# TensorE's loop rotated, with the pooled output products interleaved with the next window-strip's kv products, and the masked copies of v made on GpSimd

## The reference

```
qkv    = einsum(xw, qkv_w)                     # per 4x4 window, 384 channels
pooled = avg_pool5(qkv)                        # within the window
q, k   = relu(q), relu(k);  v = [v, 1]         # 32 heads of 8 channels: 16 full, 16 pooled
kv     = einsum('ngld,nglm->ngdm', k, v)       # per window and head, 8 x 9
out    = einsum('ngld,ngdm->nglm', q, kv)
out    = out[..., :-1] / (out[..., -1:] + 1e-15)
y      = bn(einsum(out, proj_w));  return x + y
```

## Time and profile before

| | us |
|---|---|
| median of three runs | 928.52 (928.47 to 930.1) |
| the profiled execution: its time | 930.24 |
| the profiled execution: its span, first to last instruction | 928.3 |
| mean granted TensorE clock, share of full speed | 0.993 |

### The profile page before, as it was taken

One profiled execution on the slowest core, in us unless ns is written; L12 is line 12 of the kernel. 1 busy time (PEld: TensorE's weight loads), 2 busy tenths in 40 slices (PEclk: granted clock), 3 DMA queues, 4 the chain that ended last, 5 costly groups with the idle time before them and its releaser, 6 DMA issues.

```text
span 928.3 us, 65376 instructions
## 1 busy us (share of the span) xinstructions
PE 873.8 (94%) x29282; PEld 733.4 (79%) x29282; DVE 772.3 (83%) x1625; ACT 609.5 (66%) x1542; POOL 456.0 (49%) x967
## 2 busy tenths in 40 slices
PE   0689999999999999999999999999999999999997
PEld 0578888888888888888888888888888888888885
DVE  7369989998878898998878998999887878787886
ACT  0457676767676767676766667676767676767673
POOL 1545454545454545555554545454545454545550
PEclk9999999999999999999999999999999999999998
DMA  9910000000000000000000000000000000000000
GB/s 378 431 50 17 26 17 26 17 26 17 25 19 25 26 17 26 17 26 17 26 17 26 18 26 17 26 17 27 17 26 17 25 25 18 26 17 26 18 26 27
DMA packets 15893, 38.77 MB, mean 42 GB/s; under 512 B 1888, under 2 KB 14688, under 8 KB 15456
## 3 DMA queue, kind: packets, MB, share of 16 engines
q1 hardware_dynamic: 15840, 38.26, 10.6%
HBM read 19.38 MB, written 18.87 MB: 41 GB/s over the span
## 4 chain that ended last, share of the span: by engine, by line
PE 93%; issue 3%; DVE 2%; POOL 1%; DMA 0%; ACT 0%; DVEq 0%; POOLq 0%
PE ps L611 23%; PE ps L582 19%; PE ps L538 14%; PE ps L549 9%; PE ps L556 9%; PE ps L633 7%; PE ps L627 6%; PE ps L635 4%; PE ps L558 4%; DVE stats L377 1%; DMA x_all<-x 0%; POOL hs L234 0%; DVE kvc_full L446 0%; POOL xp L234 0%; ACT o_sb L325 0%
## 5 line engine op out<-in xcount | busy, mean ns | idle before, releaser
L255 POOL TENSOR_TENSOR xn<-x_all,mean_t 128x384 f32<-128x384 f32 x96 | 79.4, 827 | 393.6 <-PE ps L558 375.1
L305 ACT ACTIVATE vm_pool<-ps,cst 128x256 f32<-128x256 f32 x576 | 225.5, 543 | 0.4 <-PE ps L549 0.4
L446 DVE TENSOR_TENSOR kvc_full<-ps,cst 128x864 f32<-128x864 f32 x192 | 193.7, 1050 | 17.8 <-PE ps L582 17.6
L446 DVE TENSOR_TENSOR kvc_pool<-ps,cst 128x864 f32<-128x864 f32 x192 | 193.2, 1048 | 0.0
L305 ACT ACTIVATE vm_full<-ps,cst 128x384 f32<-128x384 f32 x384 | 192.2, 598 | 0.9 <-PE ps L538 0.9
L312 ACT ACTIVATE q_full<-ps 128x384 f32<-128x384 f32 x96 | 47.2, 491 | 208.5 <-PE ps L556 208.5
L538 PE MATMUL ps<-wkv_sb,xn 128*128 128x128 f32 x1152 | 145.5, 276 | 23.5 <-POOL xn L256 23.5
L538 PEld LDWEIGHTS ps<-wkv_sb,xn 128*128 128x128 f32 x1152 | 144.1, 193 | 23.5 <-issue 23.5
L452 DVE SCALAR_TENSOR_TENSOR x_all<-ps,shift,x_all 128x384 f32<-128x384 f32 x96 | 59.3, 618 | 93.4 <-PE ps L633 93.2
L611 PEld LDWEIGHTS ps<-kvc_full,q_full 64*32 64x32 f32 x9216 | 99.5, 105 | 26.4 <-issue 26.3
L611 PE MATMUL ps<-kvc_pool,q_pool 64*32 64x72 f32 x9216 | 115.8, 230 | 2.1 <-issue 2.1
(11 more groups left out here) (66 smaller groups left out, 1242.2 us busy)
## 6 DMA issues: line engine op xcount, KB each, us to landing
out<-x_all SPq DMA_DIRECT2D x96, 192.0 KB, 1.9
x_all<-x SPq DMA_DIRECT2D x3, 4608.0 KB, 32.1
x_all<-x SPq DMA_DIRECT2D x6, 768.0 KB, 8.1
cst<-consts SPq DMA_DIRECT2D x1, 172.0 KB, 11.0
wkv_sb<-wkv SPq DMA_DIRECT2D x1, 128.0 KB, 10.8
o_sb<-proj SPq DMA_DIRECT2D x1, 128.0 KB, 10.4
wq_sb<-wq SPq DMA_DIRECT2D x1, 64.0 KB, 10.5
bn_sb<-bn SPq DMA_DIRECT2D x1, 2.0 KB, 10.3
```

What stands on the lines that cost most here:

```text
L255: link(pool.tensor_tensor(xr, src, mean, ALU.subtract), 1)
L305: last = act.activation(heads[:, :, e, :, 0:D], src, ACT.Copy, scale=col(mask + e))
L446: last = dve.tensor_tensor(kvc[:, g], src.to_broadcast(shape), own, ALU.mult)
```

## The change

1. TensorE's step is rotated. Before: kv(s), kv pooled(s), conv q(s), conv kv(s+1), transposes(s-1), conv kv pooled(s+1), project(s-1), out(s), out pooled(s). After: transposes(s-1), conv kv pooled(s+1), project(s-1), out(s), then out pooled(s) interleaved with kv(s+1), kv pooled(s+1), conv q(s+1), conv kv(s+2). The cyclic order is the same except for the interleaving. In it two of the six (tile, window) groups of the pooled output products (32 instructions) alternate with one tile of the full kv products (16 instructions), three times; the counts of `out_p` and `kv_f` come after the last of each.
2. The waits of that interleaved group are for `vm_f` of strip s+1 and for `y_done` of strip s-1. `y_done` no longer has its extra first count, so the strips that are waited for are the ones of before: kv(s+1) after the residual of s-1.
3. The loop of two steps is entered after steps 0 and 1 and left before steps 94 and 95, so that six step bodies stand in TensorE's program where there were four.
4. ScalarE copies full v once, to `v_full`; GpSimd makes the four masked copies from it (`masked_v`, 432 elements a partition each, the ones included), at the start of its step, ahead of `normalise_and_pool`. The pooled branch stays on ScalarE.
5. GpSimd normalises in one `tensor_scalar` instead of two `tensor_tensor`.
6. Two waits of TensorE for `km_p` and `vm_p` in `conv_q`, and a few others that later waits cover, are left out.

```diff
-                link(pool.tensor_tensor(xr, src, mean, ALU.subtract), 1)
-                pool.tensor_tensor(xn[:, p], xn[:, p], rstd, ALU.mult).then_inc(xn_ready, 1)
+                pool.tensor_scalar(xr, src, mean_t[:, s:s + 1], rstd_t[:, s:s + 1], ALU.subtract,
+                                   ALU.mult).then_inc(xn_ready, 1)
...
+            def masked_v(s):
+                pool.wait_ge(v_copied, s + 1)
+                wait(pool, kv_f, s)
+                for e in range(EF):
+                    last = pool.tensor_scalar(vm_full[:, :, e].rearrange("p t i c -> p t (i c)"),
+                                              v_full[:].rearrange("p t i c -> p t (i c)"), col(C_VF + e), None,
+                                              ALU.mult)
+                last.then_inc(vm_f, 1)
             def step(s, b, at, phase):
+                if not is_last(s):
+                    masked_v(s + 1)
...
+            def copy_v(s):
+                act.wait_ge(v_f, s + 1)
+                wait(act, vm_f, s)
+                act.activation(v_full[:].rearrange("p t i (h c) -> p t (i h) c", c=HC)[:, :, :, 0:D],
+                               ps[:, V_F, 0:TF * P].rearrange("p (t h m) -> p t h m", t=TF, m=D),
+                               ACT.Copy).then_inc(v_copied, 1)
...
+            def out_pooled_and_kv(s):
+                pe.wait_ge(vm_f, s + 2)
+                wait(pe, y_done, s)
+                pe.nop(nofuse=True)
+                groups = [(t, e) for t in range(TP) for e in range(WP)]
+                for i in range(TF):
+                    for t, e in groups[QG * i:QG * (i + 1)]:
+                        last = out_tile(True, t, e)
+                    if i == TF - 1:
+                        last.then_inc(out_p, 1)
+                    last = kv_tile(False, i)
+                last.then_inc(kv_f, 1)
...
             def step(s, p):
-                kv_products(s, False)
-                kv_products(s, True)
-                conv_q(s, p)
-                if not is_last(s):
-                    conv_kv(s + 1, 1 - p)
                 if not is_first(s):
                     transposes(s - 1)
                 if not is_last(s):
                     conv_kv_pooled(s + 1, 1 - p)
                 if not is_first(s):
                     project(s - 1)
-                out_products(s, False)
-                out_products(s, True)
+                out_products(s)
+                if is_last(s):
+                    out_products_pooled(s)
+                else:
+                    out_pooled_and_kv(s)
+                    kv_products_pooled(s + 1)
+                    conv_q(s + 1, 1 - p)
+                if not is_last(s) and not is_last(s + 1):
+                    conv_kv(s + 2, p)
```

More of the change, by code:

```diff
@@ L278, in _ @@
             normalise_and_pool(1, 1)
+            masked_v(0)
             over_strips(step)
@@ L293, in relu_k_pooled, with masked_v_pooled @@
                                ACT.Relu, scale=1 / 25.0).then_inc(km_p, 1)
[L295 to L301, removed]
-                heads = vm[:].rearrange("p t e i (h c) -> p t e (i h) c", c=HC)
-                src = ps[:, bank, 0:tiles * P].rearrange("p (t h m) -> p t h m", t=tiles, m=D)
-                for e in range(wins):
-                    last = act.activation(heads[:, :, e, :, 0:D], src, ACT.Copy, scale=col(mask + e))
-                last.then_inc(done, 1)
+            def copy_v(s):
[4 more added lines that the diff above has]
+                               ACT.Copy).then_inc(v_copied, 1)
+            def masked_v_pooled(s):
+                act.wait_ge(v_p, s + 1)
+                wait(act, kv_p, s)
+                heads = vm_pool[:].rearrange("p t e i (h c) -> p t e (i h) c", c=HC)
+                src = ps[:, V_P, 0:TP * P].rearrange("p (t h m) -> p t h m", t=TP, m=D)
+                for e in range(EP):
+                    last = act.activation(heads[:, :, e, :, 0:D], src, ACT.Copy, scale=col(C_VP + e))
+                last.then_inc(vm_p, 1)
             def relu_q(s):
@@ L587, in out_products, with kv_tile @@
-            def out_products(s, pooled):
-                q, kvc, done, bank, tiles, wins = (
-                    (q_pool, kvc_pool, out_p, OUTP, TP, WP) if pooled else
-                    (q_full, kvc_full, out_f, OUTF, TF, WF))
-                pe.wait_ge(qm_p if pooled else qm_f, s + 1)
-                pe.wait_ge(kvc_p if pooled else kvc_f, s + 1)
-                if not pooled:
-                    pe.wait_ge(kvc_p, s + 1)
-                elif not is_last(s):
-                    pe.wait_ge(km_f, s + 2)
-                    pe.wait_ge(vm_f, s + 2)
-                pe.nop(nofuse=True)
+            def kv_tile(pooled, t):
+                k, vm, bank, n = (k_pool, vm_pool, KVP, EP * KC) if pooled else (k_full, vm_full, KVF, EF * KC)
+                for r in range(G):
+                    rows = slice(H64 * r, H64 * (r + 1))
+                    for i in range(4):
+                        last = pe.matmul(ps[Q4 * i:Q4 * (i + 1), bank + r, t * n:(t + 1) * n],
+                                         k[rows, t, Q4 * i:Q4 * (i + 1)], vm[rows, t, :, i, :],
+                                         start=True, stop=True)
+                return last
@@ L614, in out_products @@
-                last.then_inc(done, 1)
+                for g in range(G):
+                    rows = slice(H64 * g, H64 * (g + 1))
+                    for c in range(4):
+                        r, w = c // QG, t * QG * wins + c % QG * wins + e
+                        last = pe.matmul(ps[Q4 * c:Q4 * (c + 1), bank + g, t * n:(t + 1) * n],
+                                         blocks[rows, 4 * t + c, Q4 * e:Q4 * (e + 1)], kvc[rows, r, w],
+                                         start=e == 0, stop=e == wins - 1)
@@ new lines, in out_tile, with kv_products, kv_products_pooled @@
+                return last
+            def kv_products(s):
+                wait(pe, y_done, s - 1)
+                pe.wait_ge(km_f, s + 1)
+                pe.wait_ge(vm_f, s + 1)
+                pe.nop(nofuse=True)
+                for t in range(TF):
+                    last = kv_tile(False, t)
+                last.then_inc(kv_f, 1)
+            def kv_products_pooled(s):
+                pe.wait_ge(vm_p, s + 1)
+                wait(pe, num_f, s)
+                pe.nop(nofuse=True)
+                for t in range(TP):
+                    last = kv_tile(True, t)
+                last.then_inc(kv_p, 1)
```

109 lines of the change are left out of this document (50 added, 59 removed).

## The result

| | before | after |
|---|---|---|
| median | 929.31 (928.47 to 931.02, 4 runs) | 1357.92 (1356.69 to 1360.28, 4 runs) |
| profiled span | 928.3 | 1356.0 |
| mean granted clock | 0.993 | 0.875 |

The ratio is 1.4606, 95% interval 1.458 to 1.4631: 46% slower, against a forecast of 919 us and a range that ended at 968. From here on a step is the distance between the starts of the q products of two strips in TensorE's timeline. From the fifth q products to the last there are 91 steps: (1342.13 - 99.85) / 91 = 13.65 us after, (914.32 - 78.12) / 91 = 9.19 before. They make 91 x 4.46 = 406 of the 427.7 us between the two spans; the fifth q products start 21.7 later (the first ones 7.9 later, and the four steps from there to the fifth 13.8 longer), and what follows the last is as long as before, 13.8 us against 13.9.

What follows compares the result with a forecast made beforehand. TensorE, busy 94% of the span, was taken as the bound. 36 steps at 9.05, 6 at 9.56 and 50 at 8.98 make 832.2 against 844.6; with 3 us for the start, 9.4 less: 919 us, range 905 to 968.

Steps and rivals of the forecast that it cites:

- M: Time of GpSimd's four masked copies of 432 elements: taken as 0.55 us each, 2.2 in all, bounds 1.60 to 3.72.
- third chain: Transposes, `to_image`, ScalarE's copy of v, GpSimd's masks, next interleaved group: 6.78 + M, 8.98 us a step.
- the forecast's own case of fast masks: Rival: with M up to 2.0 the residual binds, plain steps 8.81, those with statistics 9.05, time 911; chance 0.20.
- GpSimd becomes the bound: Rival: interleaved group waits for `vm_f` every step; 950 us at 0.65 an operation, 1053 at 0.93; chance 0.33.
- It now waits for two things that had a stage of 1.1 us more to spare before: Start of TensorE's interleaved group: its waits for the residual and the masks lose 1.1 us of slack.
- the 0.20 that ScalarE's pooled copies cost before: TensorE's wait for `vm_pool` ahead of kv pooled, 0.20 us every second step, expected to go as ScalarE loses 1.5.
- the hidden jump: TensorE's loop jump, behind 12 long conv kv instructions: priced 0 instead of 0.22 us a step.
- The normalise: GpSimd's two operations made one: loses 0.83 us, a handover and perhaps 0.5; strips 0 and 1 ready 2.2 earlier.
- The six bodies: Six cold step bodies in TensorE's program instead of four: about 1 us near the start, bounds 0 and 4.5.
- Steps with statistics: VectorE's loop through the residual, `out_p` and `own_heads`: 9.05 us in 36 steps, 9.56 in six with reductions.
- The interleaving: TensorE's pooled output and full kv products fill each other's gaps: 1.60 us for the group instead of 1.86.
- one of the rivals: Interleaving gains nothing, group 1.86 us: near 945 alone, near 928 with masks of 0.45; chance 0.08.

Runs made afterwards that it cites:

- e9_probe: The kernel before plus single GpSimd operations of 72, 432 and 864 elements behind its last strip, each waited for; 1020.38 us, one run.
- e2_tt_masks: The kernel after, with GpSimd's four masks made by `tensor_tensor` with the mask column broadcast instead of `tensor_scalar`; 1061.88 us, ratio 1.1415.
- e11_copies: The kernel after, with plain GpSimd copies in place of the masked ones, so window masking is left out; 935.66 us, ratio 1.0058.
- e4_masks_alone: The kernel before, with only the four full masked copies on GpSimd and one copy of v on ScalarE; 1405.81 us, ratio 1.5107.
- e1: The kernel after, with the four full masked copies made by ScalarE again, straight from PSUM; 937.27 us, ratio 1.0059.
- e5: e1 without interleaving: the pooled output products, then the full kv products; 931.83 us, ratio 1.0019.
- e6: e5 with the wait for the residual (`y_done`) moved behind the pooled output products; 929.76 us, ratio 0.9995.
- e10: e6 with `conv_kv` at the head of the step, so four step bodies stand in TensorE's program instead of six; 923.88 us, ratio 0.9936.
- e12_shared_masks: e10 with two of the four full masks on ScalarE and two on GpSimd by `tensor_tensor` with broadcast column; 893.67 us, ratio 0.9609.
- e13: e12_shared_masks with the interleaving put back and the wait for the residual behind the first third of the pooled output products; 904.36 us, ratio 0.9734.
- e8_late_mask_wait: The kernel after, with pooled output products in series waiting only for `v_copied`, and `vm_f` waited for ahead of the kv products; 1234.6 us, ratio 1.3274.

## Why the prediction was wrong

**The step that failed** is the price of M: "One input should need about the memset's time an element, and some of those 0.22 ... I take 0.55". It measured 1.367, outside its own bounds (0.40 to 0.93), so that M is 5.40 instead of 2.2. Both bounds came from other kinds of operation. The upper one took for granted that fewer inputs can't cost more than two, and e9_probe shows that they can: 1.37 against 1.09 at 432 elements. The Trainium skill's page "GPSIMD Engine Reference" has this order too (§ 4.1, as told in the prediction). The probe agrees for a copy (0.8 ns an element) and disagrees for `tensor_scalar` (2.5, more than `tensor_tensor`'s (2.00 - 1.09) / 432 = 2.1); by its § 3.1 I had estimated 0.65 for this operation, half of the measured.

**The form of the chain held,** with 0.2 too little in it. The forecast's third chain was 6.78 + M. Where the masks bind, e2_tt_masks gives 10.50 - 3.50 = 7.00, and after, less the 1.24 for the clock, 13.65 - 1.24 - 5.40 = 7.01. Most of the difference of 0.2 is the way from the interleaved group to q: 2.68 in e11_copies, where I had 1.60 + 0.90 = 2.50. At 7.00 + M the step is back at before's 9.19 with M = 2.19. So my own M of 2.2 would have given no gain: the steps of e11_copies that are shorter than 9.20 would have grown to it, 12.3 us together, which makes about 948 (an estimate from its 935.66 and its 91 steps).

**The price of M was not the only error.** With M = 2.02 the forecast's own case of fast masks has 911, and e11_copies took 935.66. Of these 25 us, the 45 plain steps at 9.00 instead of 8.81 make 9 and those with statistics 2; the fifth q products come 9.3 later than in before, where 3 was allowed; the last step of 11.87 makes 3, and the reduction steps about 5. Right masks alone would have left the change a little slower than before.

**The clock was in no case.** The 4.67 us between 13.65 and the forecast's 8.98 are 3.20 of M, 1.24 of the clock and 0.18 of the group; 0.05 is left over. The rival "GpSimd becomes the bound" named the mechanism, with 0.33, but its dearest figure was 1053 us at M = 3.72, and it held no loss of clock. Short of that loss it was near: for M = 3.50 its sum gives 1033, and e2_tt_masks, with that M and the clock at 1.00, came out at 1061.88.

**Slack that wasn't there, and a loop not seen.** "It now waits for two things that had a stage of 1.1 us more to spare before": true of the residual alone. `out_products` of before waits for `vm_f` of the next strip ahead of its pooled part (L601), and e4_masks_alone shows the stall there. And I counted the 0.20 that ScalarE's pooled copies cost before as a wait that the freed ScalarE would take away; with the masks on ScalarE it is a loop of 9.1 that holds every step of e1, e5, e6 and e10. That is why the rotation and the hidden jump bring so little by themselves: the mean step falls from 9.19 to ScalarE's 9.10, and the start, the end and the reductions take it back (e6_late_y_wait: same as before; e10_four_bodies: 0.6% faster). e12_shared_masks confirms the loop: with ScalarE's busy time 54 us lower over the run than in e10_four_bodies (555.9 against 609.7) the step is 8.75.

**The normalise** was taken as cheaper by more than half, with no effect other than at the start. Its 1654 ns equal the two old ones. The first kv products start at 37.52 instead of 30.09, 7.4 later where I had 2.0: 3.2 more of M, and 2.2 that I had credited to this operation.

**The six bodies** were priced at 1 us within bounds of 0 and 4.5. e10_four_bodies says 6, 2.2 of it in the last step, which I had called unchanged.

**What held:** the jump is hidden behind long matmuls (e1_act_masks has no alternation, where before had 9.06 and 9.31). The residual holds the plain steps once the masks are fast, 0.2 later than summed (9.00 in e11_copies against 8.81). Steps with statistics 9.05 forecast, 9.10 measured; with reductions 9.56 forecast, three steps of each image at 9.51 to 10.26 in e11_copies, so undersized. The forecast put the 0.80 of the earlier trace rows into six steps, but those rows count 4 such operations in the run, one an image; the other long step has seven small operations instead. ScalarE's one copy takes 0.50.

**The interleaving** was worth 0.26 a step in the forecast. From the start of the pooled output products to q it is 2.68 interleaved (e11_copies) and 711.59 - 708.92 = 2.67 in series (e12_shared_masks), so it is worth nothing, as one of the rivals said. It delays `out_p`, which VectorE's waits in e1 and e13 show, and so costs 5.4 us (e5 against e1) to 10.7 us (e12 against e13, where the wait for the residual has moved as well).

**What the change gets right** is that some of ScalarE's masks should leave it. Two of four, in the cheaper form, with no interleaving and four bodies, give 893.67 us, against 930.5 for before in the same comparison.

## What to carry to other kernels

Measure the one operation that a move depends on, by itself, before pricing it from its neighbours: fewer inputs did not mean less time on GpSimd. When work goes to another engine, go round every loop that closes through it and move only as much as leaves each of them under the bound: half of these masks moved gave 3% (e12 against e10); the kernels with all of them moved are 14% (e2_tt_masks) and 46% slower than before. An idle stretch of TensorE can cost its length and a slower restart, so a chain that binds TensorE by microseconds is dearer than its sum.

## What the runs showed of the hardware

- GpSimd, f32, 128 partitions, 432 elements: copy 0.55 us, `tensor_tensor` with a broadcast column 0.91, `tensor_tensor` 1.09, `tensor_scalar` with an immediate 1.29, with a column 1.37, with two operations 1.82. A fused pair of 384 elements (1654 ns) is no faster than two `tensor_tensor` (827 + 829).
- TensorE's granted clock was 0.50 for the 2.9 us behind stalls of 3.5 us (after) and 1.00 behind stalls of 1.62 (e2_tt_masks). In e8_late_mask_wait it fell to 0.50 shortly behind each stall of 2.0 us and behind 24 of 55 of 2.54; a step with a fall took 13.02 us, one without 11.38.
- Two more step bodies in TensorE's program cost 3.9 us near the start of the kernel and 2.2 in its last step (e6_late_y_wait against e10_four_bodies). That these are instructions met for the first time is argued, not shown.
- The gap of a hardware loop's jump (0.35 us) is gone when long matmuls are queued ahead of it: no step alternates in e1_act_masks or e10_four_bodies, nor in e12_shared_masks, where TensorE itself sets the step.
